# Row maxima of two attention heads at once on two 64-row tiles of TensorE, from three of six piece products

## The chip, the core and the metric

The kernel runs on one core of one Trainium2 chip. The metric is the device time of one execution in microseconds (us). The kernel is one program in two phases, which share the core's five engines: TensorE (PE in the rows; its weight loads are PEld), VectorE (DVE), ScalarE (ACT), GpSimd (POOL) and SyncE (SP, whose queue issues nearly all DMAs).

## What is computed

The reference is a decoder layer for x of 4 sequences of 512 tokens with 512 channels: a state-space mixer, a cross attention to a context, and a mixture of 16 experts with a shared one. The change is inside the attention:

```python
def _L0_xattn_ref(q, k, v):
    NUM_Q_HEADS = 32
    NUM_KV_HEADS = 8
    D = E // H                       # 16
    G = H // KV                      # 4 query heads share one key head
    qh = q.reshape(B, S, KV, G, D).transpose(0, 2, 3, 1, 4)
    kh = k.reshape(B, S, KV, D).transpose(0, 2, 1, 3)
    scores = jnp.einsum('bkgsd,bktd->bkgst', qh, kh) / scale
    weights = jax.nn.softmax(scores, axis=-1)
    out = jnp.einsum('bkgst,bktd->bkgsd', weights, vh)
...
x = x + _L0_attn_ref(_layernorm(x, axis=-1), ...)
x = x + _L0_xattn_ref(_layernorm(x, axis=-1), ctx_512, ctx_512)
x = x + _L0_ffn_ref(_layernorm(x, axis=-1), ...)
```

The contraction of the scores is only 16 long, in float32. The kernel cuts each float32 value of q and k into three bf16 pieces (high, middle, low) and stacks pairs of pieces on the partitions, so that one bf16 matmul with 6 x 16 = 96 rows adds up the six products that matter. For a softmax the maximum of each row is subtracted. It needs to be only near the maximum, because it cancels in the quotient.

## The kernel before

`stream_phase` handles mixer, attention and the shared expert; `experts_phase` does the routed experts after it. In `stream_phase` every engine walks the same list of **slots**, from -92 to 263. A sequence b has 64 attention slots (8 key heads of 8 slots, `UNITS`), and its mixer runs 92 slots (`LEAD`) ahead of its attention. So the mixer of sequences 1 to 3 lies in the same slots as the attention of 0 to 2, and the last 92 attention slots have no mixer beside them: a shared expert (`front`) is done there in smaller portions. The position in a sequence's mixer is called m.

In one attention slot TensorE issues, strictly in this order:

- `scores(slot)`: two heads' scores into `ps_s`, from all 99 rows of `k_stack` and `q_stack` (96 piece rows and three rows that subtract the maximum). It waits until ScalarE has taken the slot before (`s_exp`).
- half of the mixer's work (`mixer_half`), which writes into `acc`
- `max_scores(m)`, 12 slots ahead (`AHEAD`): the same products again, transposed, without the three rows, into `ps_m`. One unit is one head and two tiles of 128 query rows. It waits until VectorE has reduced the unit before (`s_max`), since `ps_m` is one buffer.
- the other half of the mixer's work
- in every second slot `products`: probabilities times values, into `ps_o`

VectorE takes each unit of `ps_m` with one reduction (`maxima`), ScalarE each unit of `ps_s` with one exponential (`probabilities`), into a ring of `PROB` = 6 buffers. When a head's eight units are reduced, GpSimd cuts the maxima into three pieces (`split_max`), TensorE turns them (`transpose_max`), and SP copies them into `q_stack` (`max_rows`).

From slot 0 on every product is cut by columns (`product`): four matmuls with 32 stationary columns each, at four column positions of the array, over all its 128 rows.

```python
for c in range(0, P, 32):
    ins = nc.tensor.matmul(dst[c:c + 32, :], stationary[:, c:c + 32], moving, start=start, stop=stop,
                           tile_position=(0, c))
```

Some transposes are 128 columns wide all the same. Before slot 0 (`tiled[0]` false) products have 128 columns.

On SP, `stack_keys` and `stack_queries` build the stacks by DMA, one per group of 16 rows, at fixed slots: keys of the first four key heads 32 slots ahead of the sequence's first slot, queries 19, 14 and 10 slots ahead, the rest in its slot 1. The mixer's weight blocks go through a ring `wring` of `RING` = 10; `freed` loads block w + 10 when block w has been used, and TensorE comes to a new block every two slots.

## Time and profile before

| | |
|---|---|
| time before, median of 3 runs (lowest, highest) | 1223.11 us (1222.42, 1224.43) |
| span of the profiled execution, first to last instruction | 1221.6 us |
| PE busy | 1172.0 us, 96% |
| DVE busy | 692.4 us, 57% |
| ACT busy | 475.3 us, 39% |
| POOL busy | 316.5 us, 26% |
| granted TensorE clock, mean | 0.996 |

Busy is the union of an engine's instructions. The end of a matmul is modelled, so the distance from one start to the next start tells its cost, not its duration. The attention begins at 186.9 us of the span, the mixer of the last sequence ends near 690 us, the last attention slot is near 892 us, and what follows is the experts' phase. The profiled execution's span is all that its page gives for its own time; the median of the timed runs is 1.5 us above it.

### The profile page before, as it was taken

The numbers are of one execution on the slowest core, as the hardware profiler recorded it, in microseconds if no ns is written. First come the engines' busy times: TensorE is split into PE (matmuls) and PEld (weight loads), VectorE is DVE, ScalarE is ACT, GpSimd is POOL, SyncE is SP. The second block draws the span as 40 slices with busy tenths as digits, with TensorE's granted clock in tenths as the row PEclk, the third lists the DMA queues.
The fourth block names the chain that finished last, engine by engine and source line by source line (L and its number), as shares of the span: only waits on it lengthen the run. The fifth ranks groups of instructions, "written<-read, shape, count | busy, mean of one in ns | idle before, by whom it ended". The sixth has DMA issues, their size and how long they took to land. (4 is left out here: it accounts for less than half of the span.)

```text
span 1221.6 us, 31126 instructions
## 1 busy us (share of the span) xinstructions
PE 1172.0 (96%) x13185; PEld 583.6 (48%) x13186; DVE 692.4 (57%) x1146; ACT 475.3 (39%) x669; POOL 316.5 (26%) x457
## 2 busy tenths in 40 slices
PE   6999999999999999999999999999999999999996
PEld 3444434444545544545645554544444444444442
DVE  4742596756787665668675777877657222222220
ACT  3321223534554453545453455555622222222221
POOL 5112311221221230231122121111102444344443
PEclk9999999999999999999999999999999999999998
DMA  8320785104284201264500146200135666678640
GB/s 195 103 88 22 184 175 112 36 16 119 62 161 91 68 29 27 78 126 102 112 20 16 68 105 94 81 3 3 72 125 179 151 180 141 163 193 242 159 88 14
DMA packets 113057, 122.17 MB, mean 100 GB/s; under 512 B 18928, under 2 KB 78448, under 8 KB 112800
## 3 DMA queue, kind: packets, MB, share of 16 engines
q1 hardware_dynamic: 101680, 98.58, 31.6%
q0 software_dynamic: 10528, 21.12, 8.7%
q8 instruction: 99, 1.62, 0.6%
q10 hardware_dynamic: 720, 0.61, 0.2%
q14 instruction: 30, 0.25, 0.1%
HBM read 94.63 MB, written 28.97 MB: 101 GB/s over the span
## 5 line engine op out<-in xcount | busy, mean ns | idle before, releaser
L680 DVE TENSOR_REDUCE mx<-ps_m 128x2 f32<-128x1024 f32 x256 | 312.9, 1222 | 193.8 <-PE ps_m L1019 189.6
L887 ACT ACTIVATE prob<-ps_s 128x1024 f32<-128x1024 f32 x256 | 262.2, 1024 | 322.7 <-PE ps_s L1019 321.9
L1019 PE MATMUL acc<-xnT,wring 128*32 128x512 f32 x1888 | 249.6, 593 | 0.6 <-DVE first_z L616 0.6
L1836 PE MATMUL ps_gu<-ring,xgT 128*128 x376 | 176.7, 593 | 1.0 <-DVE xgT L1544 1.0
L1019 PE MATMUL ps_s<-q_stack,k_stack 99*32 99x512 bf16 x2048 | 161.9, 380 | 4.4 <-ACT prob L887 3.8
L1019 PE MATMUL ps_m<-k_stack,q_stack 96*32 96x512 bf16 x1952 | 153.5, 380 | 9.6 <-DVE mx L680 8.1
L1544 DVE COPY xgT<-ps_x 128x512 f32<-128x512 f32 x47 | 32.5, 691 | 201.4 <-PE ps_x L1806 201.4
L1204 PE MATMUL ps_o<-prob,values 128*32 128x128 f32 x4096 | 138.6, 273 | 0.0
L1204 PEld LDWEIGHTS ps_o<-prob,values 128*32 128x32 f32 x4096 | 116.5, 110 | 44.4 <-issue 38.6
L1019 PEld LDWEIGHTS ps_m<-k_stack,q_stack 96*32 96x32 bf16 x1952 | 55.9, 96 | 126.9 <-issue 71.9
L1502 POOL DMA_INDIRECT out<-y,dest x47 | 74.5, 1585 | 149.4 <-DMA out<-y,dest 135.8
L1836 PEld LDWEIGHTS ps_gu<-ring,xgT 128*128 128x128 f32 x376 | 67.7, 190 | 68.2 <-issue 68.2
L1019 PEld LDWEIGHTS ps_s<-q_stack,k_stack 99*32 99x32 bf16 x2048 | 59.2, 96 | 77.6 <-issue 41.4
L1852 PE MATMUL acc<-ring,hT 128*128 x188 | 88.6, 593 | 0.9 <-ACT hT L1694 0.9
L1017 PE MATMUL acc<-xnT,wring 128*128 128x512 f32 x184 | 85.8, 605 | 2.1 <-DVE xz L598 2.0
L1019 PEld LDWEIGHTS acc<-xnT,wring 128*32 128x32 f32 x1888 | 66.1, 109 | 43.1 <-issue 6.4
L1019 PE MATMUL acc<-wring,xz 128*32 128x512 f32 x576 | 76.5, 593 | 0.0
L598 DVE SCALAR_TENSOR_TENSOR xz<-acc,convw,xz 128x511 f32<-128x511 f32 (+2 forms) x84 | 62.6, 746 | 4.0 <-ACT xz L968 2.0
L1701 ACT ACTIVATE y<-acc,share 128x512 f32<-128x512 f32 x47 | 32.3, 687 | 83.6 <-PE acc L1852 81.9
L426 POOL TENSOR_SCALAR mneg<-mx 128x16 f32<-128x16 f32 x32 | 10.2, 318 | 195.7 <-DVE mx L680 195.7
L1017 PEld LDWEIGHTS acc<-xnT,wring 128*128 128x128 f32 x184 | 34.4, 193 | 42.1 <-issue 33.0
L1489 POOL DMA_INDIRECT xg<-xn_rows,token x47 | 47.3, 1007 | 27.7 <-DVE token L1619 13.7
(282 smaller groups left out, 1180.6 us busy)
## 6 DMA issues: line engine op xcount, KB each, us to landing
ring<-in_w_experts SPq DMA_DIRECT2D x96, 256.0 KB, 5.5
wring<-in_w_in SPq DMA_DIRECT2D x80, 256.0 KB, 4.3
q_stack<-part_rows SPq DMA_DIRECT2D x96, 128.0 KB, 4.6
wring<-in_w_out SPq DMA_DIRECT2D x32, 256.0 KB, 2.9
part_rows<-part SPq DMA_DIRECT2D x20, 384.0 KB, 3.9
out<-x SPq DMA_DIRECT2D x4, 1024.0 KB, 4.9
xt<-in_x SPq DMA_DIRECT2D x14, 256.0 KB, 4.5
k_stack<-part_rows SPq DMA_DIRECT2D x48, 64.0 KB, 3.5
```

Source lines behind the costliest of these rows:

```text
L598: ins = nc.vector.scalar_tensor_tensor(out=xz[:, i, tap:], in0=bank(b, 5 + i)[:, :SEQ - tap], scalar=convw[:, i, 3 - tap:4 - tap], in1=xz[ ...
L680: nc.vector.tensor_reduce(mx[:, n % G, 2 * u:2 * u + 2], ps_m[:, :, :], AX.X, ALU.max).then_inc(s_max, 1)
L887: nc.scalar.activation(prob[:, slot % PROB, :, :], ps_s[:, :, :], ACT.Exp, scale=SCALE).then_inc(s_exp, 1)
L1017: return nc.tensor.matmul(dst, stationary, moving, start=start, stop=stop)
L1019: ins = nc.tensor.matmul(dst[c:c + 32, :], stationary[:, c:c + 32], moving, start=start, stop=stop, tile_position=(0, c))
L1204: ins = nc.tensor.matmul(out_rows.rearrange("p (t i) -> p t i", i=VW), values[:, t, g, :], weights[:, a, :, :], start=(t == 0 and r == 0), ...
L1489: pool.indirect_dma_start(out=xg[:, n % XG, :], out_offset=None, in_=xn_rows[:, :], in_offset=bass.IndirectOffsetOnAxis(ap=token[:, n:n + ...
L1502: pool.indirect_dma_start(out=out[:, :], out_offset=bass.IndirectOffsetOnAxis(ap=dest[:, n:n + 1], axis=0), in_=y[:, n % YB, :], in_offset ...
L1544: nc.vector.tensor_copy(xgT[:, p, :], ps_x[p][:, :]).then_inc(s["txc"], 1)
L1701: nc.scalar.activation(y[:, n % YB, :], ps_y[p][:, :], ACT.Copy, scale=share[:, n:n + 1]).then_inc(s["yc"], 1)
L1836: ins = nc.tensor.matmul(ps_gu[p][:, :], xgT[:, p, k * P:(k + 1) * P], weights(own)[:, k * 2 * F:(k + 1) * 2 * F], start=(k == 0), stop=(k ...
L1852: ins = nc.tensor.matmul(ps_y[p][:, :], hT[:, p, k * P:(k + 1) * P], weights(own)[:, WUP + k * D:WUP + (k + 1) * D], start=(k == 0), stop= ...
```

## The change

The maxima are taken from the three leading piece products alone (high x high, high x middle, middle x high), which is 3 x 16 = 48 rows. A unit is now two heads and one tile of 128 query rows: the even head's 48 rows stand on partitions 0 to 47, the odd head's on partitions 64 to 111, and each head's four column tiles are issued at its own row position (0 or 64), into its own half of `ps_m`. A unit is 8 matmuls before and after: before each on 96 rows x 32 columns, now on 48 rows x 32 columns of a tile 64 rows high. Scores still need all six products. To leave the 48 rows of both heads where they must be, even and odd heads have different row orders, with one group of 16 rows blank (zero in `q_stack`), and the keys are stacked twice, once in each order. The score matmuls now have 115 rows instead of 99.

```diff
-    RING = 10
+    RING = 8
...
-    Q_PART = (0, 0, 0, 1, 1, 2)
-    K_PART = (0, 1, 2, 0, 1, 0)
-    KQ = len(Q_PART) * DH
+    EVEN_Q, EVEN_K = (0, 0, 1, 2, 0, 1, None), (0, 1, 0, 0, 2, 1, None)
+    ODD_Q, ODD_K = (0, 2, 1, None, 0, 1, 0), (2, 0, 1, None, 0, 0, 1)
+    KQ = len(EVEN_Q) * DH
     KM = KQ + 3
+    LEADING = 3 * DH
+    HALF_ROWS = P // 2
...
-    PROB = 6
+    PROB = 5
...
-        k_stack = sb("k_stack", [KM, G, SEQ], BF16)
+        k_stack = sb("k_stack", [P, 2, G, SEQ], BF16)
...
-                for i, p in enumerate(K_PART):
-                    sp.dma_start(k_stack[i * DH:(i + 1) * DH, 4 * h:4 * h + 4, :], rows[p][:, 4 * h:4 * h + 4, :]
-                                 ).then_inc(s_kst[h], 16)
+                for odd, parts in enumerate((EVEN_K, ODD_K)):
+                    for i, p in enumerate(parts):
+                        if p is not None:
+                            sp.dma_start(k_stack[i * DH:(i + 1) * DH, odd, 4 * h:4 * h + 4, :],
+                                         rows[p][:, 4 * h:4 * h + 4, :]).then_inc(s_kst[h], 16)
...
-            nc.gpsimd.memset(k_stack[KQ:KM, :, :], 1.0).then_inc(s_ones, 1)
+            nc.gpsimd.memset(k_stack[96:P, :, :, :], 1.0).then_inc(s_ones, 1)
...
+                    if m == 14 and b == 0:
+                        pool.wait_ge(s_val, G)
+                        nc.gpsimd.memset(k_stack[32:64, 1, :, :], 0.0).then_inc(s_ones, 1)
+                        pool.wait_ge(s_ones, 2)
+                    if m == 16 and b == 0:
+                        nc.gpsimd.memset(q_stack[96:P, 0::2, :], 0.0).then_inc(s_blank, 1)
+                        pool.wait_ge(s_blank, 1)
+                    if m == 18 and b == 0:
+                        nc.gpsimd.memset(q_stack[32:64, 1::2, :], 0.0).then_inc(s_blank, 1)
+                        pool.wait_ge(s_blank, 2)
...
-                nc.vector.tensor_reduce(mx[:, n % G, 2 * u:2 * u + 2], ps_m[:, :, :], AX.X, ALU.max).then_inc(s_max, 1)
+                pair, t = divmod(u, TB)
+                columns = mx[:, n % G, :].rearrange("p (r t) -> p r t", t=TB)
+                nc.vector.tensor_reduce(columns[:, 2 * pair:2 * pair + 2, t], ps_m[:, :, :], AX.X, ALU.max
+                                        ).then_inc(s_max, 1)
...
-                for i in range(2):
-                    r, t = u // 2, 2 * (u % 2) + i
-                    ins = product(ps_m[:, i, :], q_stack[0:KQ, g * R + r, t * P:(t + 1) * P], k_stack[0:KQ, g, :],
-                                  start=True, stop=True)
+                pair, t = divmod(u, TB)
+                wide = 32 if tiled[0] else P
+                for c in range(0, P, wide):
+                    for i in range(2):
+                        rows = slice(HALF_ROWS * i, HALF_ROWS * i + LEADING)
+                        ins = nc.tensor.matmul(ps_m[c:c + wide, i, :],
+                                               q_stack[rows, g * R + 2 * pair + i, t * P + c:t * P + c + wide],
+                                               k_stack[rows, i, g, :], start=True, stop=True,
+                                               tile_position=(HALF_ROWS * i, c))
                 ins.then_inc(s_mm, 1)
```

`stack_queries` is changed in the same way: where even and odd heads have the same piece one DMA copies both, elsewhere each parity has its own half-size DMA, 8 DMAs in place of 6. In the experts' phase each expert's share is given at least one tile of 128 slots, and the register that holds an expert's end is declared to be at least 1; no operation is added.

On TensorE, in attention slots 1 and 2 with the mixer beside them, the order of the program was this (`x8` is eight matmuls in a row, `32x512` the output of one):

```order
L1019 MATMUL ps_s<-q_stack,k_stack 32x512 x8
L1019 MATMUL acc<-xnT,wring 32x512 x4
L1019 MATMUL ps_m<-k_stack,q_stack 32x512 x8
L1019 MATMUL acc<-xnT,wring 32x512 x4
L1019 MATMUL ps_s<-q_stack,k_stack 32x512 x8
```

and it is this with the change:

```order
L1049 MATMUL ps_s<-q_stack,k_stack 32x512 x8
L1049 MATMUL acc<-xnT,wring 32x512 x4
L1219 MATMUL ps_m<-k_stack,q_stack 32x512 x8
L1049 MATMUL acc<-xnT,wring 32x512 x4
L1049 MATMUL ps_s<-q_stack,k_stack 32x512 x8
```

Nothing moved: the eight matmuls of a maximum unit stand in the same place between two mixer products, and only their row position and height differ.

On SP, in slot 1 of the first sequence's attention, the last group of queries and the second half of the keys were stacked like this:

```order
L258 DMA wring<-in_w_out 128x512 x2
L302 DMA q_stack<-part_rows 16x8x512 x6
L293 DMA k_stack<-part_rows 16x4x512 x6
L258 DMA wring<-in_w_out 128x512
L314 DMA gain_rows<-dtr 16x128 x4
```

and with the change like this:

```order
L315 DMA q_stack<-part_rows 16x8x512
L319 DMA q_stack<-part_rows 16x4x512 x2
L315 DMA q_stack<-part_rows 16x8x512
L319 DMA q_stack<-part_rows 16x4x512
L315 DMA q_stack<-part_rows 16x8x512 x2
L319 DMA q_stack<-part_rows 16x4x512
L302 DMA k_stack<-part_rows 16x4x512 x12
L263 DMA wring<-in_w_out 128x512
L331 DMA gain_rows<-dtr 16x128 x4
```

The queries take 8 DMAs where they took 6 and the keys 12 where they took 6, so what follows on this queue is issued eight DMAs later.

On GpSimd, ahead of the first sequence's `bsb` (an input of the scan), the order was:

```order
L513 TENSOR_TENSOR dtx<-dtx,dta 128x128
L514 TENSOR_TENSOR dtx<-dtx,dtl 128x128
L463 TENSOR_TENSOR rstd<-var_eps,half 128x8
L412 COPY values<-keys 128x4x16 x8
L524 TENSOR_TENSOR bsb<-gains,bsb 128x512 x2
L529 TENSOR_TENSOR csb<-state,csb 128x512 x2
```

and now it is:

```order
L530 TENSOR_TENSOR dtx<-dtx,dta 128x128
L531 TENSOR_TENSOR dtx<-dtx,dtl 128x128
L480 TENSOR_TENSOR rstd<-var_eps,half 128x8
L429 COPY values<-keys 128x4x16 x8
L537 MEMSET k_stack 32x4096
L540 MEMSET q_stack 32x16x512
L543 MEMSET q_stack 32x16x512
L551 TENSOR_TENSOR bsb<-gains,bsb 128x512 x2
L556 TENSOR_TENSOR csb<-state,csb 128x512 x2
```

Three fills are new between the values and `bsb`, once per execution. The fill of `k_stack` further up, ahead of the first `dtu`, was 4096 columns on 3 partitions and is 8192 columns on 32.

## Rows read from the trace of the kernel before

**Rows 1.** Page: span; part 5, costliest groups (busy, mean ns, idle, releaser)
```profile
span 1221.6 us, 31126 instructions
PE 1172.0 (96%) x13185; PEld 583.6 (48%) x13186; DVE 692.4 (57%) x1146; ACT 475.3 (39%) x669; POOL 316.5 (26%) x457
...
L680 DVE TENSOR_REDUCE mx<-ps_m 128x2 f32<-128x1024 f32 x256 | 312.9, 1222 | 193.8 <-PE ps_m L1019 189.6
```

**Rows 2.** Windows: length, busy us (and count) of PE, PEld, DVE, ACT, POOL
```profile
186.00:692.00 506.00, 496.21 (x8007) 258.93 (x8005) 343.51 (x431) 235.90 (x292) 107.55 (x203) 1.00 0.32 72
692.00:892.00 200.00, 192.28 (x3511) 95.86 (x3511) 148.79 (x235) 112.28 (x130) 33.76 (x85) 1.00 0.26 63
```

**Rows 3.** Timeline of PE, 479 to 488 us: start, length, instruction
```profile
479.77 0.68 PE L1019 MATMUL ps_s<-q_stack,k_stack 99*32 99x512 bf16 x8
480.38 0.66 PE L1076 MATMUL ps_t<-ident,xt 128*128 128x128 f32 x4
480.96 1.06 PE L1019 MATMUL acc<-wring,xz 128*32 128x512 f32 x8
481.84 0.62 PE L1019 MATMUL ps_m<-k_stack,q_stack 96*32 96x512 bf16 x8
482.28 1.04 PE L1019 MATMUL acc<-wring,first_z 128*32 128x512 f32 x8
483.14 0.62 PE L1019 MATMUL ps_s<-q_stack,k_stack 99*32 99x512 bf16 x8
...
485.73 1.05 PE L1204 MATMUL ps_o<-prob,values 128*32 128x128 f32 x32
486.60 0.62 PE L1019 MATMUL ps_s<-q_stack,k_stack 99*32 99x512 bf16 x8
```

**Rows 4.** Units of ps_m in 186 to 692 us: PE matmuls and their number
```profile
L1019 PE MATMUL ps_m<-k_stack,q_stack x1304: 377/379/390, 188.6 to 690.8; 96*32 96x512 bf16 x187
```

**Rows 5.** Waits of PE, 186 to 692 us: total us, times, longest
```profile
PE ps_m L1019 <- DVE mx L680: 3.6, 4, 0.9
```

**Rows 6.** Timeline of PE around 163 and 185 us, products not yet cut
```profile
163.08 0.60 PE L1040 MATMUL ps_t<-ident,xz 128*128 128x128 f32 x4
163.52 1.02 PE L1017 MATMUL acc<-xnT,wring 128*128 128x512 f32 x2
...
185.46 0.60 PE L1017 MATMUL ps_m<-k_stack,q_stack 96*128 96x512 bf16 x2
185.90 1.02 PE L1017 MATMUL acc<-xnT,wring 128*128 128x512 f32 x2
186.85 0.61 PE L1019 MATMUL ps_s<-q_stack,k_stack 99*32 99x512 bf16 x8
```

**Rows 7.** Timeline of all engines, 795 to 798 us
```profile
795.10 0.61 PE L1019 MATMUL ps_s<-q_stack,k_stack 99*32 99x512 bf16 x8
...
795.74 0.61 PE L1019 MATMUL ps_m<-k_stack,q_stack 96*32 96x512 bf16 x8
795.77 1.02 ACT L887 ACTIVATE prob<-ps_s 128x1024 f32<-128x1024 f32 x1 [0.72 <-PE ps_s L1019]
...
796.18 1.05 PE L1204 MATMUL ps_o<-prob,values 128*32 128x128 f32 x32
796.40 1.22 DVE L680 TENSOR_REDUCE mx<-ps_m 128x2 f32<-128x1024 f32 x1 [0.72 <-PE ps_m L1019]
...
797.05 0.61 PE L1019 MATMUL ps_s<-q_stack,k_stack 99*32 99x512 bf16 x8
...
797.68 0.61 PE L1019 MATMUL ps_m<-k_stack,q_stack 96*32 96x512 bf16 x8
```

**Rows 8.** Reductions of ps_m in 692 to 892 us, and waits of PEld there
```profile
L680 DVE TENSOR_REDUCE mx<-ps_m x82: 1180/1224/1226, 691.2 to 869.7; 128x2 f32<-128x1024 f32 x82
...
PEld ps_m L1019 <- DVE mx L680: 30.3, 51, 1.5
```

**Rows 9.** Window 356 to 380 us, columns as in rows 2
```profile
356.00:380.00 24.00, 24.00 (x384) 11.83 (x380) 21.51 (x27) 13.12 (x18) 4.65 (x9) 1.00 0.49 96
```

**Rows 10.** Timeline of POOL, 20 to 84 us
```profile
23.31 3.51 POOL L484 MEMSET k_stack<- 3x4096 bf16 x1
...
34.46 2.51 POOL L412 COPY values<-keys 128x64 f32<-128x64 f32 x8
79.69 2.49 POOL L524 TENSOR_TENSOR bsb<-gains,bsb 128x512 f32<-128x512 f32 x2 [42.71 <-DMA gains<-gain_rows]
```

**Rows 11.** Timeline of SP, 385 us on, and SP's longest wait (us, times, longest)
```profile
385.77 2.74 SPq L302 DMA_DIRECT2D q_stack<-part_rows  x6
388.61 2.72 SPq L293 DMA_DIRECT2D k_stack<-part_rows  x6
...
SPq L308 <- ACT mT L1005: 261.4, 29, 24.0
```

**Rows 12.** Page, part 6: issues, count, KB each, median us to landing
```profile
wring<-in_w_in SPq DMA_DIRECT2D x80, 256.0 KB, 4.3
```

More of the change, by code:

```diff
@@ L61, in stream_phase @@
     L = G - 1
-    Q_PART = (0, 0, 0, 1, 1, 2)
-    K_PART = (0, 1, 2, 0, 1, 0)
-    KQ = len(Q_PART) * DH
+    EVEN_Q, EVEN_K = (0, 0, 1, 2, 0, 1, None), (0, 1, 0, 0, 2, 1, None)
+    ODD_Q, ODD_K = (0, 2, 1, None, 0, 1, 0), (2, 0, 1, None, 0, 0, 1)
+    KQ = len(EVEN_Q) * DH
     KM = KQ + 3
+    LEADING = 3 * DH
+    HALF_ROWS = P // 2
+    Q_LOADS = sum(1 if a == o else (a is not None) + (o is not None) for a, o in zip(EVEN_Q, ODD_Q))
+    K_LOADS = sum(a is not None for a in EVEN_K + ODD_K)
     UNITS = 8
@@ L298, in stack_queries @@
                     sp.wait_ge(s_sc, PERIOD * (b - 1) + 16 * (c + 1))
+                else:
+                    sp.wait_ge(s_blank, 2)
                 sp.wait_ge(s_prow, 16 * (5 * b + c + 2))
                 rows = dram["part_rows"][c + 1].rearrange("(j d) i t -> i d j t", d=DH)
-                for i, p in enumerate(Q_PART):
-                    sp.dma_start(q_stack[i * DH:(i + 1) * DH, c * 8:(c + 1) * 8, :], rows[p]).then_inc(s_qst[c], 16)
+                for i, (even, odd) in enumerate(zip(EVEN_Q, ODD_Q)):
+                    dst = q_stack[i * DH:(i + 1) * DH, c * 8:(c + 1) * 8, :]
+                    if even == odd:
+                        sp.dma_start(dst, rows[even]).then_inc(s_qst[c], 16)
+                        continue
+                    for at, p in enumerate((even, odd)):
+                        if p is not None:
+                            sp.dma_start(dst[:, at::2, :], rows[p][:, at::2, :]).then_inc(s_qst[c], 16)
             def max_rows(n):
@@ L1170, in scores @@
                     r = u % 2 * 2 + i
-                    ins = product(ps_s[:, i, :], k_stack[:, g, t * P:(t + 1) * P], q_stack[:, g * R + r, :],
-                                  start=True, stop=True)
+                    ins = product(ps_s[:, i, :], k_stack[0:KM, i, g, t * P:(t + 1) * P],
+                                  q_stack[0:KM, g * R + r, :], start=True, stop=True)
                 ins.then_inc(s_sc, 1)
@@ L1595, in _ @@
             V.then(nc.vector.tensor_scalar(count[:, :], count[:, :], -P, None, ALU.bitwise_and))
-            V.then(nc.vector.tensor_copy(tiles[:, 1:1 + E], count[:, :]))
+            V.then(nc.vector.tensor_scalar(tiles[:, 1:1 + E], count[:, :], float(P), None, ALU.max))
             V.then(nc.vector.tensor_tensor_scan(bounds[:, :], onesf[:, :], tiles[:, :], 0.0, ALU.mult, ALU.add))
@@ L1893, in build @@
         nc.sbuf_tensor("identb", [P, P], BF16) as identb,
-        nc.sbuf_tensor("wring", [P, 10, 512], F32) as wring,
+        nc.sbuf_tensor("wring", [P, 8, 512], F32) as wring,
         nc.sbuf_tensor("th", [P, 2, 512], F32) as th,
```

16 lines of the change are left out of this document (8 added, 8 removed).

## The prediction

> **What bounds the kernel now.** I read the page first: its groups of instructions give PE 1172.0 us busy of a span of 1221.6 us, DVE 692.4 us [rows 1]. Busy time of PE is modelled, so I then cut the span into stretches [rows 2]. In 186 to 692 us attention and mixer share PE, and it is busy for 496.21 of 506 us. The timeline there [rows 3] shows no holes: eight matmuls of a maximum unit start 0.44 us ahead of what follows (481.84 to 482.28), a mixer product takes 0.86 us (482.28 to 483.14), `products` 0.87 us (485.73 to 486.60). So here the start-to-start distance is the price, and any time taken out of PE's stream comes out of the span. Only 4 times did PE stand still for the reduction, 3.6 us in all [rows 5].
>
> The stretch of 692 to 892 us is another case. The mixer is gone, DVE is busy for 148.79 of 200 us [rows 2], and the timeline [rows 7] shows a ring of waits: maximum unit at 795.74, its reduction from 796.40 for 1.22 us to 797.62, the next unit at 797.68. That ring is 1.94 us long, of which 0.66 us run from the unit's first matmul to the reduction. Inside it PE has `ps_s` 0.43 us, then waits some 0.21 us (797.05 + 0.43 to 797.68), then the unit, then `ps_o`. PE's weight loads for `ps_m` were held up by the reduction 51 times there, of 82 reductions [rows 8]. The experts' phase after 892 us and the first 150 us contain no maximum unit.
>
> **What the change does to a maximum unit.** One unit is two rounds of four column tiles now, each round 512 columns: 0.44 / 2 = 0.22 us. If the two heads' tiles run side by side, one round is enough, and 0.22 us is saved. The rate of issue is no hindrance: `products` passes 32 matmuls in 0.87 us, 27 ns each [rows 3], so eight need 0.22 us at most.
>
> What no row of before shows is PE going from tiles over all 128 rows to tiles of 64 rows, and back. The nearest rows are changes of column width. With cut products around it, `ps_s` to `ps_t` takes 480.38 - 479.77 = 0.61 us where `ps_s` alone needs 0.43, and `ps_t` to `acc` 480.96 - 480.38 = 0.58 us [rows 3] where the same four transposes between wide products take 163.52 - 163.08 = 0.44 us [rows 6]: 0.18 us to go in, 0.14 us to come out. From two wide `acc` products to the first cut `ps_s` it is 186.85 - 185.90 = 0.95 us against 0.86: 0.09 us [rows 6]. So a change of width costs 0.09 to 0.18 us, and going and coming 0.23 to 0.32 us.
>
> The Trainium skill (TensorEngine Tiling (Array Packing), Key Properties) says that changing the tiling mode, not just the tile, drains TensorE, and lists 128x32 and 64x32 as different modes; by that rule each maximum unit would pay twice. The trace agrees for changes of column width, with the 0.09 to 0.18 us above; for a change of row height no run yet shows it. By the rule the unit gains nothing while PE is the bound; without it 0.22 us.
>
> The price of a row change is bounded by nothing (0) and by the widest column change (0.32 us for both). I take the lower part, 0.09 in and 0.14 out: what enters and leaves the unit is mostly a float32 `acc` product, as in the two cheap rows, and a maximum unit has no second round of 128-wide weights. To that come about 0.05 us by which eight tiles start one after another (an estimate: `ps_m` x8 is 0.62 us long [rows 3] and one matmul 0.379 [rows 4], so the second round's last tile starts 0.24 us in, 0.02 us after its round began; for eight tiles at 7 ns each it is 0.05). A unit then holds PE for 0.09 + 0.22 + 0.05 + 0.14 = 0.50 us instead of 0.44: **+0.06 us**. The saved round and the two changes nearly cancel; the break-even is (0.22 - 0.05) / 2 = 0.085 us per change.
>
> **The sum.**
> - 186 to 692 us: 1304 matmuls are 163 units [rows 4]. Some 158 have PE full on both sides: 158 x 0.06 = +9.5 us. The few that wait for the reduction gain about 0.2 each: -1 us.
> - 12 units ahead of slot 0, uncut: 0.44 us now (185.46 to 185.90 [rows 6]), 0.09 + 0.22 + 0.14 = 0.45 then: 0.
> - 692 to 892 us, 81 units. For the 51 that wait, the reduction starts sooner, 0.66 - 0.22 = 0.44 us after the first matmul; the 0.21 us of waiting shrinks, though a change of 0.09 that it hid comes out. PE's own work in the ring becomes 0.43 + 0.09 + 0.41 + 0.87 = 1.80 us against 1.94, and the ring by way of DVE 1.94 - 0.22 = 1.72: the slot takes 1.80, -0.14 each, -7 us. The other 30 pay 0.06: +2 us.
> - Sum +9.5 - 1 - 7 + 2 = +3.5 us. On the profiled execution's span of 1221.6 us that is 1225.1; the median of the runs lies 1.5 us over that span, so I give **1227 us** for the median.
>
> **The edits costed at nothing.**
> - The reduction reads the same 1024 columns and writes two values: 1222 ns either way [rows 1]. Scores with 115 rows for 99: matmuls with 96, 99 and 128 rows differ in no start distance.
> - DMAs: 6 took 2.74 us, 0.46 each [rows 11]. Keys add 6 x 0.46 = 2.7 us per half, queries 2 x 0.46 = 0.9 us per group: 2 x 2.7 + 4 x 0.9 = 9 us of SP's queue per sequence. The worst place is slot 1, with 20 DMAs, 9.2 us; behind them stand `freed` and the maxima's rows, which are due at slot 5, four slots or some 12 us later. SP stood waiting for the maxima alone 261.4 us [rows 11]. If that cover were gone, the next head's scores would start late by up to 3.7 us, once or twice per sequence.
> - The ring of 8: block w + 8 is asked for when w is used, 14 slots ahead of its use, before it was 18. 14 slots of over 2.5 us are 35 us against 4.3 us to landing [rows 12]. Across two sequences the lead is 7 slots, over 17 us.
> - Five probability buffers: the exponential of an odd slot now needs a `products` issued two slots earlier instead of four, but it waits for scores that PE issues after it anyway. Nothing.
> - GpSimd: 4096 columns took 3.51 us [rows 10]. The first fill grows to 8192, +3.5 us; three new ones are 3.5 + 7 + 7 = 17.5 us. The copies end at 34.46 + 8 x 2.5 = 54.5 us; so GpSimd is through at 54.5 + 3.5 + 17.5 = 75.5 us, and its next work started at 79.69. Cover 4 us. If the strided fills are slower, `bsb`, the scan and PE behind them slip by the excess, once.
>
> **Rivals.**
> - **A: row height changes free of charge.** A unit is 0.22 us instead of 0.44. 158 x 0.22 = 35 us; but where VectorE is busy 21.51 of 24 us [rows 9], as in about 8 slots for each of three sequences, little more than half of it can be had, so 32 us. In 692 to 892 us: the 1.94 us ring becomes 1.75, held by ScalarE (0.67 from `ps_s` to its start, 1.02, 0.06 back, all in [rows 7]): 81 x 0.18 = 14 us. Total -46 us: **1177 us**. For it: no row rules it out, and rows of 96, 99 and 128 follow each other without a loss. Against it: the price of column changes. The Trainium skill (TensorEngine Tiling (Array Packing), Theoretical Speedup) gives up to 2x for a small dimension of at most 64, which is this case; by that alone the time would be this rival's, and no run shows it yet. Chance 0.32.
> - **B: slower, at the upper price.** Each unit pays 0.32 us or more for the two changes, plus the 0.05: 158 x (0.22 + 0.05 + 0.32 - 0.44 = 0.15) = +24 us, 51 units about 0, 30 x 0.15 = +4: 1250 us. If the two row tiles also took turns, 0.22 us more each in 158 units, 1285. It decides from 0.1 us per change on. Speaks for it: the 0.18 us row. Against it: that row has wide weights to load. Chance 0.10.
> - **C: near balance (forecast).** 0.085 us per change is the break-even, and the rows say 0.09 to 0.14. Its own range is 1215 to 1238. Chance 0.58.
>
> **How the numbers follow.** A measurement of this kernel can tell about 0.2% (2.4 us) from no change. C's middle is 3.5 us above before, with some 8 us to either side: faster 0.25, same 0.27, slower 0.48 of it. Faster: 0.32 + 0.58 x 0.25 = 0.46. Same: 0.16. Slower: 0.58 x 0.48 + 0.10 = 0.38. The range must reach into A, since leaving it out drops 0.32: from 1176, the better half of A left out, to 1240. It leaves out about 0.2.
>
> **What would show it.** In C the timeline of 186 to 692 us has a unit of `ps_m` 0.36 to 0.43 us ahead of the next `acc`, and `acc` 0.95 us or more ahead of `ps_m` where it was 0.86. In A, 0.22 and 0.86. In B, over 0.43 and over 1.0. In all, a reduction starts about 0.44 us after the unit's first matmul (0.66 before), and waits of PE for `mx` after 692 us nearly vanish. I am wrong in the mechanism if a unit of eight takes 0.44 us of streaming, if PE waits for `q_stack` or `wring`, or if `bsb` starts after 80 us.

## The result, and the profile after

The changed kernel took **1240.89 us** (median of 4 runs, 1234.02 to 1248.07) against 1223.77 us for the kernel before in the same comparison (1222.42 to 1231.04). The ratio is 1.012, with a 95% interval of 1.0082 to 1.0158: slower by 1.2% (the medians themselves are 17.1 us or 1.4% apart). The forecast was 1227 us, so the sign was right and the size 14 us short. Of the stated range, 1176 to 1240 us, the median passes the upper end by 0.9 us; the ratio times the 1223.11 us that the forecast started from is 1237.8 us, inside it. Its profiled execution took 1234.02 us, with a span of 1232.2 us.

The page of the changed kernel, its span, part 1, and two groups of part 5, which answer to [rows 1]:

```profile
span 1232.2 us, 31213 instructions
PE 1170.7 (95%) x13184; PEld 519.5 (42%) x13186; DVE 707.6 (57%) x1146; ACT 474.9 (39%) x669; POOL 339.6 (28%) x460
...
L709 DVE TENSOR_REDUCE mx<-ps_m 128x2 f32<-128x1024 f32 x256 | 313.4, 1224 | 188.0 <-PE ps_m L1219 187.2
...
L1219 PE MATMUL ps_m<-k_stack,q_stack 48*32 48x512 bf16 (+1 forms) x1976 | 104.7, 387 | 8.7 <-DVE mx L709 8.2
```

PE is busy for no longer than before (1170.7 us for 1172.0), and the reduction costs what it did. Two things stand out that don't follow from the maximum units: VectorE is busy 15 us longer with the same 1146 instructions, and GpSimd 23 us longer with three instructions more.

The same two windows as in [rows 2], and a third one in the prologue:

```profile
186.00:692.00 506.00, 496.99 (x7781) 203.60 (x7780) 345.15 (x428) 232.67 (x290) 108.69 (x206) 1.00 0.33 79
692.00:892.00 200.00, 192.83 (x3647) 89.12 (x3642) 155.65 (x242) 113.15 (x132) 34.24 (x86) 1.00 0.26 69
30.00:60.00 30.00, 20.08 (x42) 8.50 (x41) 22.50 (x23) 8.62 (x15) 25.35 (x19) 0.83 0.26 70
```

In the first window PE gets through 7781 matmuls instead of 8007 while it is just as busy; in the second through 3647 instead of 3511. A good part of both is only where the windows lie, since slot 0 comes 12 us later in this run and the products ahead of it are not cut in four. In the third, PE is busy for 20.08 of 30 us at a granted clock of 0.83; before, it was busy for all of the 30 us, at 1.00. The same window before:

```profile
30.00:60.00 30.00, 30.00 (x71) 13.30 (x70) 22.79 (x37) 9.32 (x16) 6.56 (x15) 1.00 0.40 105
```

A table by stage makes a sum of that. I took the start of the first `ps_s` matmul of slots 0 and 160 and of the last row of `ps_o` matmuls (64 of them) from each trace; the mixer leaves PE near slot 160. Microseconds of the profiled execution:

| run | slot 0 starts at | slots 0 to 160 | slots 160 to the last `ps_o` row | from there to the end | span |
|---|---|---|---|---|---|
| before | 186.9 | 496.3 | 210.2 | 328.3 | 1221.6 |
| after | 199.0 | 500.2 | 202.4 | 330.6 | 1232.2 |
| difference | +12.1 | +3.9 | -7.8 | +2.3 | +10.6 |
| predicted | 0 | +8.5 | -5 | 0 | +3.5 |

The two stages with maximum units sum to -3.9 us: **the attention got faster, where the forecast had it 3.5 us slower, and the kernel lost the time before slot 0**, where the forecast had nothing.

**A maximum unit.** Timeline of PE in the changed kernel, to be read beside [rows 3]:

```profile
481.96 1.04 PE L1049 MATMUL acc<-wring,xz 128*32 128x512 f32 x8
482.94 0.41 PE L1219 MATMUL ps_m<-k_stack,q_stack 48*32 48x512 bf16 x8
483.27 1.07 PE L1049 MATMUL acc<-wring,first_z 128*32 128x512 f32 x8
484.16 0.62 PE L1049 MATMUL ps_s<-q_stack,k_stack 115*32 115x512 bf16 x8
```

The eight matmuls are one round: the row is 0.41 us long, where one matmul is 0.387 on the mean, and the eight start within 0.024 us. From the unit to the next product it is 483.27 - 482.94 = 0.33 us, 0.22 of streaming and 0.11 more. From the product ahead to the unit it is 482.94 - 481.96 = 0.98 us where 0.86 is usual: 0.12. The product behind takes 0.89, 0.02 or 0.03 too long. So the change of row height costs 0.12 on the way in and some 0.13 out (0.11 and 0.02): 0.98 + 0.33 + 0.89 = 2.20 us. At the place in [rows 3] it was 0.88 + 0.44 + 0.86 = 2.18, and with 0.86 ahead 2.16: 0.02 to 0.04 us more for a unit.

**After slot 160.** PE, ScalarE and VectorE in the changed kernel, to be read beside [rows 7]:

```profile
805.61 0.41 PE L1219 MATMUL ps_m<-k_stack,q_stack 48*32 48x512 bf16 x8
805.73 1.02 ACT L917 ACTIVATE prob<-ps_s 128x1024 f32<-128x1024 f32 x1 [0.91 <-PE ps_s L1049]
...
806.10 1.23 DVE L709 TENSOR_REDUCE mx<-ps_m 128x2 f32<-128x1024 f32 x1 [0.82 <-PE ps_m L1219]
...
806.84 0.62 PE L1049 MATMUL ps_s<-q_stack,k_stack 115*32 115x512 bf16 x8
807.38 0.11 PEld L1219 LDWEIGHTS ps_m<-k_stack,q_stack 48*32 48x32 bf16 x8 [0.43 <-DVE mx L709]
807.38 0.41 PE L1219 MATMUL ps_m<-k_stack,q_stack 48*32 48x512 bf16 x8
```

The reduction starts 0.49 us after the unit's first matmul (0.66 before), and the next unit comes 1.77 us after this one (1.94 before). By way of VectorE that is 0.49 + 1.23 + 0.05 us, and the weight loads do end their wait with the reduction. But PE's own work is as long: 0.54 from `ps_s` to the unit (0.43 and 0.11 or 0.12 for the change of height), 0.34 for the unit, 0.89 for the product behind it. Which of the two holds the slot shows where the reduction is done early, as 8 us later:

```profile
811.49 1.23 DVE L709 TENSOR_REDUCE mx<-ps_m 128x2 f32<-128x1024 f32 x1
...
813.03 0.62 PE L1049 MATMUL ps_s<-q_stack,k_stack 115*32 115x512 bf16 x8
813.58 0.11 PEld L1219 LDWEIGHTS ps_m<-k_stack,q_stack 48*32 48x32 bf16 x8 [0.43 <-issue]
813.58 0.41 PE L1219 MATMUL ps_m<-k_stack,q_stack 48*32 48x512 bf16 x8
```

The reduction ended at 812.72, 0.86 us ahead of the unit, and the unit still comes 0.55 us after `ps_s`. Before, that distance was 0.63 where the reduction ended 0.06 us ahead of the unit, and 0.43 where PE did not wait [rows 7]. So PE no longer waits in such a slot: its own work sets the 1.77 us, with VectorE done just in time.

**The start.** GpSimd in the changed kernel, which answers to [rows 10]:

```profile
22.55 6.92 POOL L501 MEMSET k_stack<- 32x8192 bf16 x1
...
37.13 2.83 POOL L429 COPY values<-keys 128x64 f32<-128x64 f32 x8
40.02 3.75 POOL L537 MEMSET k_stack<- 32x4096 bf16 x1
43.83 7.09 POOL L540 MEMSET q_stack<- 32x8192 bf16 x1
50.97 7.09 POOL L543 MEMSET q_stack<- 32x8192 bf16 x1
```

VectorE at the same time, where it makes the residual rows `x` and `xt` and then the taps of the convolution:

```profile
39.32 0.55 DVE L604 TENSOR_SCALAR x<-xt,keep 128x512 f32<-128x512 f32 x1
39.78 0.54 DVE L606 TENSOR_SCALAR xt<-xt,mv,rstd 128x512 f32<-128x512 f32 x1
40.23 3.82 DVE L604 TENSOR_SCALAR x<-xt,keep 128x512 f32<-128x512 f32 x1
43.97 7.22 DVE L606 TENSOR_SCALAR xt<-xt,mv,rstd 128x512 f32<-128x512 f32 x1
51.12 2.30 DVE L625 SCALAR_TENSOR_TENSOR xz<-acc,convw,xz 128x511 f32<-128x511 f32 x3
```

And PE:

```profile
39.96 3.60 PE L1047 MATMUL acc<-xnT,wring 128*128 128x512 f32 x8
53.47 5.84 PE L1047 MATMUL acc<-xnT,wring 128*128 128x512 f32 x8 [9.92 <-DVE xz L625]
```

Before, the last of these operations and PE's products at this place were:

```profile
38.17 0.53 DVE L579 TENSOR_SCALAR xt<-xt,mv,rstd 128x512 f32<-128x512 f32 x1
```

```profile
42.88 7.03 PE L1017 MATMUL acc<-xnT,wring 128*128 128x512 f32 x16
```

Read them together. A TENSOR_SCALAR that takes 0.55 us takes 3.82 when it starts 0.21 us into a fill of 3.75, and 7.22 when it starts 0.14 us into one of 7.09: it ends 0.28 and 0.27 us after the fill. One gets through between two fills and no more. Behind them wait the taps (51.12), which read `acc` in PSUM; PE needs that buffer back and stands still for 9.92 us. Then its next eight products take 5.84 us instead of 3.60: from 47.6 to 57.8 us the granted clock is 0.50, the lower of the two levels (2.4 and 1.2 GHz), and 1.00 on either side. The fills thus cost 9.92 + 2.24 = 12.2 us here. That slot 0 is late by 12.1 us is the same number partly by chance. PE came to this place 2.9 us sooner than before (39.96 for 42.88): its first eight products, at 15.82, took 3.70 us, before 5.01 us at 17.43. And it lost another 2.8 us on the way to slot 0, among them a second stretch at the lower clock, from 105.6 to 112.4 us (before, one half as long), and a wait of 1.72 us at 162.72 (before 0.58). Run 9 below, which has the early start but no fill over these operations, reaches slot 0 at 186.2, 12.8 us sooner than this one. VectorE's extra 15 us are also here: 3.3 and 6.7 us in these two, and 5.2 in a 128x4 operation that took 6.59 us under the first fill, at 22.90, and 1.34 before. That one held up nothing that PE waited for: in run 1 it took 0.20 us, and what follows on VectorE (`keep`, at 37.79) came no sooner, since it waits for GpSimd's `rstd`.

### The profile page after: what moved, and what is told of

The parts are those of the page before. It is cut to its first block and busy times, and to the rows that moved or that the text cites. A ratio compares the mean times of both kernels' runs of the same rounds, so it can differ in the third digit from the quotient of the medians.

```text
span 1232.2 us, 31213 instructions
## 1 busy us (share of the span) xinstructions
PE 1170.7 (95%) x13184; PEld 519.5 (42%) x13186; DVE 707.6 (57%) x1146; ACT 474.9 (39%) x669; POOL 339.6 (28%) x460
## 5 line engine op out<-in xcount | busy, mean ns | idle before, releaser
L709 DVE TENSOR_REDUCE mx<-ps_m 128x2 f32<-128x1024 f32 x256 | 313.4, 1224 | 188.0 <-PE ps_m L1219 187.2
L1049 PE MATMUL ps_s<-q_stack,k_stack 115*32 115x512 bf16 x2048 | 159.7, 380 | 4.7 <-ACT prob L917 4.7
L1237 PEld LDWEIGHTS ps_o<-prob,values 128*32 128x32 f32 x4096 | 113.5, 110 | 46.3 <-issue 43.9
L1219 PE MATMUL ps_m<-k_stack,q_stack 48*32 48x512 bf16 (+1 forms) x1976 | 104.7, 387 | 8.7 <-DVE mx L709 8.2
L1219 PEld LDWEIGHTS ps_m<-k_stack,q_stack 48*32 48x32 bf16 (+1 forms) x1976 | 28.6, 89 | 179.5 <-issue 130.7
L1049 PEld LDWEIGHTS ps_s<-q_stack,k_stack 115*32 115x32 bf16 x2048 | 55.2, 97 | 79.2 <-issue 42.8
L1049 PEld LDWEIGHTS acc<-xnT,wring 128*32 128x32 f32 x1888 | 48.3, 108 | 52.3 <-issue 34.9
L443 POOL TENSOR_SCALAR mneg<-mx 128x16 f32<-128x16 f32 x32 | 10.2, 319 | 188.6 <-DVE mx L709 188.2
```

The lines of the kernel that those rows point to most:

```text
L709: nc.vector.tensor_reduce(columns[:, 2 * pair:2 * pair + 2, t], ps_m[:, :, :], AX.X, ALU.max).then_inc(s_max, 1)
L1219: ins = nc.tensor.matmul(ps_m[c:c + wide, i, :], q_stack[rows, g * R + 2 * pair + i, t * P + c:t * P + c + wide], k_stack[rows, i, g, :], ...
L1237: ins = nc.tensor.matmul(out_rows.rearrange("p (t i) -> p t i", i=VW), values[:, t, g, :], weights[:, a, :, :], start=(t == 0 and r == 0), ...
```

## The experiments

Every ratio below is to the kernel before on the same chip: 1227.17 us for runs 1 to 4, 1222.76 us for runs 5 to 7, 1223.47 us for runs 8 and 9. Some of the expectations give 493 and 212 us for two stages of before; the table above has 496.3 and 210.2 for them, and it is the table that holds. I name each run's stages by the columns of the table above.

**1. The changed kernel again**, unaltered, since 1234 to 1248 us is a wide spread, and to see whether the loss stands in the same place.

```diff
(no edit of the changed kernel)
```

> The changed kernel once more, unaltered, to see whether its loss has the same places on another chip. Two theories for the first 199 us, where its profiled execution was 12 us behind: (port) GpSimd's fills of k_stack and q_stack, which ended at 58 us, held up two VectorE TENSOR_SCALARs (3.82 and 7.22 us where they took 0.54 before), and PE ran dry for 10 us and then at half clock; then this trace shows the same two long operations under the fills, slot 0 some 12 us later than before (186.9), and the ratio is 1.01 to 1.015. (ring) the weight ring of 8 in place of 10 makes PE wait for a block; then PE's first long wait here is for wring, and the two VectorE operations are long only by chance. Slots 0 to 160 should take 500 us (493 before), slots 160 to the end 203 us (212 before).

Measured: 1243.21 us, ratio 1.0143 [1.0104, 1.0182]. Slots 0 to 160 took 500.2 us and slots 160 on 202.4, as in the first profile; slot 0 started at 204.9. VectorE and PE there:

```profile
40.50 3.81 DVE L606 TENSOR_SCALAR xt<-xt,mv,rstd 128x512 f32<-128x512 f32 x1
44.23 7.22 DVE L604 TENSOR_SCALAR x<-xt,keep 128x512 f32<-128x512 f32 x1
51.38 7.22 DVE L606 TENSOR_SCALAR xt<-xt,mv,rstd 128x512 f32<-128x512 f32 x1
```

```profile
60.87 5.63 PE L1047 MATMUL acc<-xnT,wring 128*128 128x512 f32 x8 [14.33 <-DVE xz L625]
```

Here three of VectorE's eight residual operations were left when the fills began, not two, and each met a fill. The hole is 14.33 us for 9.92, the eight products behind it take 2.03 us too long, and slot 0 is late by 18.0 us. The other 1.6 us are lost later, and no single place accounts for them. PE's head start of the first profile is missing in this execution of the same kernel (its first eight products took 5.26 us, at 17.25). VectorE's operations began 0.4 us later against the fills, which made the difference between two and three of them: 4.2 us of the step from 12.1 to 18.0. Most of the rest is the head start. That this makes the spread of 1234 to 1248 us is likely, but only two executions were looked at.

**2. The three later fills wait until VectorE has done its first taps.** This tells the fills from every other cause of the late start.

```diff
                     if m == 14 and b == 0:
                         pool.wait_ge(s_val, G)
+                        pool.wait_ge(s_conv, 1)
                         nc.gpsimd.memset(k_stack[32:64, 1, :, :], 0.0).then_inc(s_ones, 1)
```

> The changed kernel with one wait more: GpSimd's three new fills begin only when VectorE has done the first taps (semaphore conv_done at 1), that is after the TENSOR_SCALARs of the residual. The first fill (8192 columns at 22 us) stays where it was. Port theory: the long VectorE operations at 40 to 51 us go back to 0.54 us, PE has no hole there, slot 0 comes 10 to 13 us sooner than in the changed kernel, and the time is about 1222 to 1228. Ring theory: no change against the changed kernel, 1238 to 1242.

Measured: 1227.85 us, ratio 1.0004 [0.9973, 1.0035]. The fills now lie over the taps. GpSimd, then VectorE:

```profile
44.18 3.50 POOL L538 MEMSET k_stack<- 32x4096 bf16 x1 [3.62 <-DVE xz L626]
47.74 6.92 POOL L541 MEMSET q_stack<- 32x8192 bf16 x1
```

```profile
41.28 0.55 DVE L607 TENSOR_SCALAR xt<-xt,mv,rstd 128x512 f32<-128x512 f32 x1
...
43.98 2.31 DVE L626 SCALAR_TENSOR_TENSOR xz<-ps_s,convw,xz 128x511 f32<-128x511 f32 x3
46.20 0.68 DVE L637 SCALAR_TENSOR_TENSOR xz<-th,xz 128x512 f32<-128x512 f32 x1
46.80 2.31 DVE L626 SCALAR_TENSOR_TENSOR xz<-ps_s,convw,xz 128x511 f32<-128x511 f32 x3
```

All eight residual operations take 0.54 or 0.55 us, and the taps under the fills keep their 2.31. PE has no hole between 35 and 60 us. Slot 0 started at 192.4, 6.5 us sooner than in the first profile of the changed kernel (10 to 13 were expected) and 12.5 sooner than in run 1. Against before it is 5.6 us late, though PE was 2.3 us ahead at 40.58. The granted clocks are 0.90 in 60 to 110 us and 0.95 in 150 to 187 us (before 0.97 and 1.00), which is 0.07 x 50 + 0.05 x 37 = 5.4 us of the engine's time. PE also waited 1.96 us at 86.19 and 2.29 us at 154.53 (before 0.39 and 0.58); neither is for an operation under a fill. This profiled execution is the slowest of the ten (1235.41 us); the ratio, over all of them, says that the edit gives back the loss, with one wait. What remains is within the interval.

**3. The fills alone**, in the kernel before: neither the stack of two orders nor the row tiles.

```diff
             nc.gpsimd.memset(k_stack[KQ:KM, :, :], 1.0).then_inc(s_ones, 1)
             pool.wait_ge(s_ones, 1)
+            nc.gpsimd.memset(k_stack[32:64, :, :], 0.0).then_inc(s_ones, 1)
+            pool.wait_ge(s_ones, 2)
...
+                    if m == 14 and b == 0:
+                        pool.wait_ge(s_val, G)
+                        nc.gpsimd.memset(k_stack[32:64, :, :], 0.0).then_inc(s_ones, 1)
+                        pool.wait_ge(s_ones, 3)
+                    if m == 16 and b == 0:
+                        nc.gpsimd.memset(q_stack[64:96, 0::2, :], 0.0).then_inc(s_blank, 1)
+                        pool.wait_ge(s_blank, 1)
+                    if m == 18 and b == 0:
+                        nc.gpsimd.memset(q_stack[32:64, 1::2, :], 0.0).then_inc(s_blank, 1)
+                        pool.wait_ge(s_blank, 2)
```

(The rows filled are overwritten by the stacks' DMAs, which wait for `s_ones` and `s_blank` as in the changed kernel.)

> The kernel before, with nothing of the change but fills of the same lengths at the same places in GpSimd's order (4096 more columns ahead of the first dtu, then 4096, 8192 and 8192 after the values), on rows of the stacks that are overwritten later. Ring of 10, six products, no row tiles. Port theory: it pays what the changed kernel pays at the start, +12 to +15 us, 1236 to 1240, with PE dry between 43 and 55 us. Ring theory: 1223 to 1225.

Measured: 1245.25 us, ratio 1.0147 [1.0095, 1.0198]. Slots 0 to 160 and 160 on are those of before (496.1 and 210.3 us), slot 0 starts at 204.6. The time is 5 us over the 1236 to 1240 that were expected, as the hole is that of run 1 and not of the first profile. VectorE and PE:

```profile
40.62 3.81 DVE L596 TENSOR_SCALAR xt<-xt,mv,rstd 128x512 f32<-128x512 f32 x1
44.35 7.22 DVE L594 TENSOR_SCALAR x<-xt,keep 128x512 f32<-128x512 f32 x1
51.50 7.22 DVE L596 TENSOR_SCALAR xt<-xt,mv,rstd 128x512 f32<-128x512 f32 x1
```

```profile
60.99 3.44 PE L1034 MATMUL acc<-xnT,wring 128*128 128x512 f32 x4 [14.88 <-DVE xz L615]
```

Four fills that nobody needs make the kernel before as slow as the changed one. With run 2 that settles the start: the three fills at this place are needed for the loss, and the fills are enough for it.

**4. A change of row height without the second row tile.** Maxima from three products of 48 rows, one head after the other, all at row 0. This leaves out the second-order products of the maxima. It measures the price of the change by itself, and whether two row positions matter.

```diff
-    Q_PART = (0, 0, 0, 1, 1, 2)
-    K_PART = (0, 1, 2, 0, 1, 0)
+    Q_PART = (0, 0, 1, 0, 1, 2)
+    K_PART = (0, 1, 0, 2, 1, 0)
...
-                    ins = product(ps_m[:, i, :], q_stack[0:KQ, g * R + r, t * P:(t + 1) * P], k_stack[0:KQ, g, :],
+                    ins = product(ps_m[:, i, :], q_stack[0:48, g * R + r, t * P:(t + 1) * P], k_stack[0:48, g, :],
```

> The kernel before, with the order of the six products changed so that the leading three stand on the first 48 partitions, and maximum units that read these 48 rows alone (the maxima come from three products): still one head at a time, two rounds of four column tiles at row position 0, nothing else changed. It has the change of row height without the second head beside it. Theory 'price of the row change' (0.11 us to go in, 0.12 to come out, 0.02 after): every unit with PE full pays 0.25 us on top of its 0.44, 158 x 0.25 = 40 us, and 6 to 10 us more in the other units: 1265 to 1275. Theory 'two row positions at once': the 0.11 and 0.12 us come from running both halves of the array together, tiles of 48 rows at one position cost nothing extra: 1223, and acc follows ps_m after 0.44 us as before.

Measured: 1274.02 us, ratio 1.0383 [1.0331, 1.0434]. Timeline of PE:

```profile
479.06 1.04 PE L1019 MATMUL acc<-wring,first_z 128*32 128x512 f32 x8
480.03 0.61 PE L1019 MATMUL ps_m<-k_stack,q_stack 48*32 48x512 bf16 x8
480.57 1.06 PE L1019 MATMUL acc<-wring,xz 128*32 128x512 f32 x8
481.46 1.06 PE L1204 MATMUL ps_o<-prob,values 128*32 128x128 f32 x32
```

0.97 us into the unit (+0.11), 0.54 us for it (0.44 + 0.10), 0.89 behind it (+0.03): about 0.25 us for each unit, the same as with two row positions. Slots 0 to 160 took 534.1 us instead of 496.3, +37.8, which is 0.24 a slot. (Two stretches of 3.4 us at the lower clock, at 240 and 455 us, are in it and account for up to 3.4 us, which leaves at least 0.21.) So the price is that of going from 128 rows to few and back, and a second row position adds nothing. It also shows what the second row tile saves: it takes a round of 0.22 us out of these 0.25.

**5. The ring of eight and five probability buffers alone**, in the kernel before.

```diff
-    RING = 10
+    RING = 8
...
-    PROB = 6
+    PROB = 5
...
-        nc.sbuf_tensor("wring", [P, 10, 512], F32) as wring,
+        nc.sbuf_tensor("wring", [P, 8, 512], F32) as wring,
```

> The kernel before with only the weight ring cut from 10 to 8 blocks and the probability buffers from 6 to 5. In the changed kernel PE's first products came 1.6 us and the steady stream 2.9 us sooner than before; if that is because two of ten block loads no longer stand ahead of the rest in the first 12 us of the DMA queues, this run is 1 to 3 us faster than before (1220 to 1222) with first acc<-wring product near 15.8 us. If the shorter rings cost waits, PE waits for wring or ACT for ps_o appear and it is 1224 to 1228. If both count for nothing, 1223.

Measured: 1223.87 us, ratio 1.0002 [0.998, 1.0023], slots 0 to 160 and 160 on as before within 0.2 us and slot 0 at 188.3. Nothing, as forecast. The sooner first products that the shorter ring might have explained did not come (5.13 us for the first eight, at 16.96). Run 4, with the rings of before, has them (3.70 us, at 16.53), and run 1, with the shorter ones, has not. So they differ from execution to execution and are not the change's.

**6. Row tiles only after the mixer**, and all four fills late. The changed kernel, with the six products up to the unit where the mixer is gone, the 176th; the leading three and two row tiles from there on.

```diff
-            nc.gpsimd.memset(k_stack[96:P, :, :, :], 1.0).then_inc(s_ones, 1)
-            pool.wait_ge(s_ones, 1)
...
                         pool.wait_ge(s_val, G)
+                        pool.wait_ge(s_conv, 1)
+                        nc.gpsimd.memset(k_stack[96:P, :, :, :], 1.0).then_inc(s_ones, 1)
+                        pool.wait_ge(s_ones, 1)
...
+                if m < SLOTS - LEAD + AHEAD:
+                    for i in range(2):
+                        ins = product(ps_m[:, i, :], q_stack[0:KQ, g * R + 2 * pair + i, t * P:(t + 1) * P],
+                                      k_stack[0:KQ, i, g, :], start=True, stop=True)
+                    ins.then_inc(s_mm, 1)
+                    return
```

> The changed kernel with all four fills after the first taps, and with row tiles only for the maximum units issued from slot 164 on, where no mixer stands beside the attention; earlier units use all six products over 112 rows, two heads and one tile of rows as before in two rounds of four column tiles. If the price of the row change is what costs in slots 0 to 160 (+7 us there) and the gain of 9 us after slot 160 is that of the shorter round, this takes both: 1223 - 9 - (0 to 3 for the start) = 1211 to 1215. If the gain after slot 160 came from elsewhere (queries' or keys' timing), it is 1220 or more.

Measured: **1219.13 us, ratio 0.9959 [0.9939, 0.9979]**, the best of all: 0.4% faster than the kernel before. Slots 0 to 160 took 496.1 us (before 496.3), slots 160 on 203.5 (before 210.2), slot 0 started at 188.4. The stages promise -6.9 us and the median gives -3.6 against the kernel before of its comparison, -5.0 by the ratio. The 1211 to 1215 us expected were not reached: they counted on 9 us after slot 160, and the table has 7.8.

**7. The same with the six products throughout**: new stack, more DMAs, small rings and late fills without row tiles.

```diff
-                if m < SLOTS - LEAD + AHEAD:
+                if True:
```

> The changed kernel's stacks, DMAs, rings and unit order, with all four fills after the first taps, and no row tiles at all: every unit takes all six products over 112 rows. This is everything of the change but the row tiles. If they alone make the difference after slot 0, slots 0 to 160 take 493 us and the rest 212 as before, and the time is 1220 to 1224. If the doubled key DMAs or the shorter lead of the rings cost, it is above 1226 and the trace shows PE or ACT waiting for q_stack, k_stack or wring.

Measured: 1228.52 us, ratio 1.0021 [0.9998, 1.0045]. All middle stages are those of before to 0.2 us (496.1 and 210.3), and PE waited for neither stack nor `wring`, so the stacking, its added DMAs and the rings cost nothing there, as forecast. The time still misses the 1220 to 1224 us that were expected. The end, from the last `ps_o` on, took 334.9 us instead of 328.3 in this execution, the slowest of its twelve (1230.62 us). Between runs 6 and 7 only the row tiles differ: 9.4 us of medians, 6.8 of them in slots 160 on.

**8. The three later fills where the change put them, in 20 pieces of 1024 columns.** If VectorE waits for a whole instruction of GpSimd, shorter ones must cut each wait.

```diff
-                        nc.gpsimd.memset(k_stack[32:64, 1, :, :], 0.0).then_inc(s_ones, 1)
+                        for j in range(3):
+                            nc.gpsimd.memset(k_stack[32:64, 1, 2 * j:2 * j + 2, :], 0.0)
+                        nc.gpsimd.memset(k_stack[32:64, 1, 6:8, :], 0.0).then_inc(s_ones, 1)
...
-                        nc.gpsimd.memset(q_stack[96:P, 0::2, :], 0.0).then_inc(s_blank, 1)
+                        for j in range(7):
+                            nc.gpsimd.memset(q_stack[96:P, 4 * j:4 * j + 4:2, :], 0.0)
+                        nc.gpsimd.memset(q_stack[96:P, 28:32:2, :], 0.0).then_inc(s_blank, 1)
```

(The third fill is cut as the second.)

> The changed kernel with its three later fills cut into 20 pieces of 1024 columns, at the same place in GpSimd's order and with no new wait. In the runs so far each VectorE TENSOR_SCALAR that met a fill ended with that fill (3.8 us, 7.2 us), and one of them got through between two fills. If the port is held for one instruction, each of the last three or four TENSOR_SCALARs now waits for one piece, some 0.95 us in place of 7.2, so PE's hole shrinks to 0 to 2 us, slot 0 comes at about 190, and the time is 1223 to 1230. If GpSimd keeps it while it has work queued, the first of them lasts until the pieces end (to 58 us), as bad as before: 1240 to 1248.

Measured: 1223.16 us, ratio 0.9997 [0.9976, 1.0018]. VectorE and PE:

```profile
40.25 1.25 DVE L612 TENSOR_SCALAR xt<-xt,mv,rstd 128x512 f32<-128x512 f32 x1
41.42 1.25 DVE L610 TENSOR_SCALAR x<-xt,keep 128x512 f32<-128x512 f32 x1
42.59 1.25 DVE L612 TENSOR_SCALAR xt<-xt,mv,rstd 128x512 f32<-128x512 f32 x1
43.76 2.30 DVE L631 SCALAR_TENSOR_TENSOR xz<-acc,convw,xz 128x511 f32<-128x511 f32 x3
```

```profile
46.10 3.70 PE L1053 MATMUL acc<-xnT,wring 128*128 128x512 f32 x8 [2.21 <-DVE xz L631]
```

The same three operations meet the same work in the same place, and each takes 1.25 us instead of 3.8 or 7.2. PE's hole is 2.21 us instead of 14, its granted clock is 1.00 from 20 to 150 us, and slot 0 starts at 188.6. The first fill was left whole, so it is not what the other runs lost by. The length of the single instruction sets the price, not the number of columns filled.

**9. The changed kernel with all four fills late** and row tiles in all units: what the change would have been without the loss at the start.

```diff
-            nc.gpsimd.memset(k_stack[96:P, :, :, :], 1.0).then_inc(s_ones, 1)
-            pool.wait_ge(s_ones, 1)
...
                         pool.wait_ge(s_val, G)
+                        pool.wait_ge(s_conv, 1)
+                        nc.gpsimd.memset(k_stack[96:P, :, :, :], 1.0).then_inc(s_ones, 1)
+                        pool.wait_ge(s_ones, 1)
```

> The changed kernel with all four fills after the first taps, row tiles for every unit. Beside the hybrid (row tiles only from slot 164 on) it has the price of the row change in the 160 slots where PE is full: slots 0 to 160 take 500.2 us (496.1 in the hybrid), the slots after them 202.4 as in the changed kernel. So 3 to 5 us slower than the hybrid and about 0 to 2 us faster than the kernel before: ratio 0.998 to 1.001. If the price were a matter of the start alone, it would equal the hybrid, 0.996.

Measured: 1222.76 us, ratio 0.9997 [0.998, 1.0015]. Slot 0 at 186.2, slots 0 to 160 500.2 us, slots 160 on 203.4 (202.4 in the changed kernel; a stretch of 3.4 us at the lower clock, at 701 us, is in it). Attention is 2.9 us shorter than before by its stages, and the ratio shows 0.4 of it.

## Why the prediction was right on the row height and wrong at the start

**The forecast case, near balance: right as a mechanism.** The saved round is whole (0.22 us; eight tiles side by side), and the row change costs 0.12 us in and 0.13 us out, where I had said 0.09 and 0.14. Its sign in the attention was wrong all the same: +3.5 us was forecast and -3.9 us measured, by two small terms that follow. For its estimate the forecast took changes of column width, and those turned out to be near in size. The Trainium skill (TensorEngine Tiling (Array Packing), Key Properties) says that a change of mode drains TensorE: runs 1 and 4 agree, with 0.25 us for both changes.

**One term of that sum was too big.** "About 0.05 us by which eight tiles start one after another" is 0.02 us in the trace, and it is part of the 0.13 us out. The unit then costs 0.12 + 0.22 + 0.13 = 0.47 us, +0.03 and not +0.06, and slots 0 to 160 took +3.9 us and not +8.5 (0.024 a slot). The distance from a unit to the next `acc`, 0.33 us, lies for the same reason below the 0.36 to 0.43 us that I had named for this case.

**After slot 160: right in the ring, too small in the sum.** I had said that PE's own work would hold the slot, at 1.80 us; it does, at 1.77. VectorE's way round, which I had put at 1.72 us, is 1.77 too, since the reduction starts 0.49 us after the unit and not 0.44. The sign that the waits for `mx` would nearly vanish did not come: PE's weight loads still end 56 of them with the reduction, 29.6 us in all (before 51 and 30.3). The 1.77 us are -0.17 for each of 51 units, -8.7 us, and with the other 30 at +0.03 instead of +0.06 the sum is -7.8, as the stage has it, for -5. So the gain of a waiting unit was put 0.03 us too low, and the loss of the others 0.03 us too high.

**The failed step is "GpSimd: ... Cover 4 us".** It was wrong in two ways.
- I read `8 x 2.5` out of a row whose length is that of all eight copies together [rows 10]. They end at 37 us and not at 54.5, so the fills start at 40 us, on top of VectorE's residual operations, and not behind them.
- I asked only when GpSimd would be late for its own next work (`bsb`). That cover was better than I had said: GpSimd was through at 58.06 us, and `bsb` started at 89.63. That is past the 80 us that I had named as a sign of being wrong, but 31.6 us after GpSimd was free: it came 9.9 us later than before, as did the rest of the chain behind PE's hole. What I did not ask is who else is held up while a fill runs. The cost lay on VectorE, and from there on PE. The Trainium skill states this rule (SBUF — State Buffer, "SBUF: two separate sides"): VectorE and GpSimd share a pair of SBUF ports, and of a GpSimd operation and a VectorE one in a two-port mode, which `tensor_scalar` can enter, the one that starts first has it for the whole instruction. The trace agrees, with 3.82 and 7.22 us under fills of 3.75 and 7.09; the prediction had not weighed that rule.

Runs 2, 3 and 8 show it from three sides: the same fills elsewhere cost nothing beyond the noise, the same fills alone cost 1.5%, the same columns in pieces leave a hole of 2.2 us and no loss beyond the noise.

**The rest at nothing: right.** Five buffers and a ring of eight (run 5), the doubled keys with their DMAs (run 7), reductions of 1224 ns for 1222, scores with 115 rows for 99 (`ps_s` to the next product is 0.43 us in both).

**Rival A, row height free of charge: false.** It wanted 0.22 us for a unit and 0.86 ahead of it; the trace has 0.33 and 0.98. **Rival B, slower at the upper price: false.** It wanted over 1.0 us ahead of the unit and over 0.43 for it. What made the kernel slower was none of the rivals. That it came out slower, as forecast, is thus luck, and the fills alone brought it to the edge of the range: without the fills over VectorE's operations it is the kernel before again (run 9, 1222.76 us for 1223.47).

**Open.** Runs 6 and 9 gain less than their stages say, by 2 to 3 us, and run 7 has +0.2% with unchanged middle stages. Part of that is that the profiled executions of runs 6 and 7 are the slowest of their twelve. In them the difference lies behind the last `ps_o`: 332.3, 330.0 and 334.9 us (runs 6, 9 and 7) for 328.3. But runs 3 and 5, whose code there is that of before, have 336.0 and 328.7, and run 8, with the new stacks, 329.0. In this phase `xg` and `out` move by indirect DMAs, and it varies from execution to execution; whether the new stacks add to it, one profile of each kernel doesn't tell.

## What to carry to other kernels

A filler on an idle engine is free only if nobody who shares something with that engine is on the path: ask for GpSimd's long instructions what VectorE does under them, and cut them or put them where VectorE does what is not held up (here SCALAR_TENSOR_TENSOR). Here a change of tile height cost TensorE about 0.12 us each way, so a unit between taller ones must save more than 0.25 us by it; where TensorE waits anyway, it pays. (Many such units in a row would share one change; no run here tried that.) Split such a change by stage: here it gained after the mixer and lost within it, and only the version that uses it in one of the two stages is faster.

## What the runs showed of the hardware

- **GpSimd fills and VectorE.** A TENSOR_SCALAR float32 from SBUF to SBUF of 0.55 us takes 3.8 us under a MEMSET of 4096 columns and 7.2 us under one of 8192, 1.25 us under one of 1024 (changed kernel, runs 1, 3 and 8). SCALAR_TENSOR_TENSOR was not held up, neither from PSUM (2.31 us for three) nor from SBUF (0.68 us, run 2). GpSimd is hardly held up itself: 7.09 for 6.92 us.
- **A clock behind a hole.** PE stood still for 9.92 us; meanwhile the granted clock went from 1.00 to 0.50 (47.6 to 57.8 us), and its next eight products took 5.84 us for 3.60. After 2.21 us (run 8) the clock stayed at 1.00, and they took 3.70.
- **Row height.** From 128 rows to 48 and back costs 0.11 or 0.12 us in and 0.12 or 0.13 us out, with one row position as with two; 96, 99, 112 and 115 rows among 128 cost nothing (0.43 or 0.44 us from such a unit to the next product).
- **Repeatability.** The middle stages repeat to 0.2 us over the executions of the same code where the granted clock is 1.00 throughout; a stretch of 3.4 us at the lower clock adds about 1 us (runs 6 and 9, 203.5 and 203.4 us for 202.4). What else differs between executions lies before slot 0 and after the attention.
